# Two stacked attention layers on one core: the reciprocal row sums travel by DMA through device memory instead of through TensorE, and the normalisation comes four steps later

## The reference

```python
# layer 0
q = einsum('oc,bcn->bon', Wq, xf) + bq          # 32 rows
k = einsum('oc,bcn->bon', Wk, xf) + bk          # 32 rows
v = einsum('oc,bcn->bon', Wv, xf) + bv          # 256 rows
attn = softmax(einsum('bci,bcj->bij', q, k), axis=1)
x = gamma * einsum('bcn,bnm->bcm', v, attn) + xf
# layer 1
theta = conv1x1(x, theta_w, theta_b)            # 32 rows, 4096 positions
phi = maxpool2(conv1x1(x, phi_w, phi_b))        # 32 rows, 1024 positions
g = maxpool2(conv1x1(x, g_w, g_b))              # 128 rows, 1024 positions
attention = softmax(theta^T phi, axis=-1)
y = gamma * (out_w @ (g @ attention^T) + out_b) + x
```

## Time and profile before

| | |
|---|---|
| median of 3 executions | 2790.31 us (2786.36 to 2790.55) |
| profiled execution, own time | 2785.08 us |
| its span | 2783.3 us |
| PE busy | 2693.6 us (97%) |
| POOL busy | 1956.3 us (70%) |
| DVE busy | 2004.2 us (72%) |
| ACT busy | 1745.2 us (63%) |

### The profile page before, as it was taken

One profiled execution on the slowest core, in us unless ns is written; L12 is line 12 of the kernel. 1 busy time (PEld: TensorE's weight loads), 2 busy tenths in 40 slices (PEclk: granted clock), 3 DMA queues, 4 the chain that ended last, 5 costly groups with the idle time before them and its releaser, 6 DMA issues.

```text
span 2783.3 us, 39336 instructions
## 1 busy us (share of the span) xinstructions
PE 2693.6 (97%) x12260; PEld 2159.1 (78%) x12260; DVE 2004.2 (72%) x3303; ACT 1745.2 (63%) x3171; POOL 1956.3 (70%) x1544
## 2 busy tenths in 40 slices
PE   7999999999999999998999999999899999999988
PEld 5788888877688888887778888888767888888866
DVE  7677777767767777776776777777676777777665
ACT  5566666666756666666765566666676666666657
POOL 3677777767767767776786767777577677777768
PEclk9999999999999999999999999999999999999989
DMA  2000000012110000001211000000121000000011
GB/s 86 1 16 24 16 24 16 16 39 69 61 38 16 24 16 16 16 16 38 69 65 35 24 16 16 16 16 16 46 76 61 16 16 16 16 16 16 16 46 61
DMA packets 43194, 85.03 MB, mean 31 GB/s; under 512 B 2672, under 2 KB 2800, under 8 KB 42992
## 3 DMA queue, kind: packets, MB, share of 16 engines
q1 hardware_dynamic: 35360, 68.17, 7.2%
q10 hardware_dynamic: 7632, 14.36, 1.8%
HBM read 48.96 MB, written 33.55 MB: 30 GB/s over the span
## 4 chain that ended last, share of the span: by engine, by line
PE 87%; DVE 4%; issue 3%; ACT 3%; POOL 2%; DMA 0%; POOLq 0%; ACTq 0%; DVEq 0%
PE o_ps L821 18%; PE o_ps L824 18%; PE o_ps L825 18%; PE s_ps L798 10%; PE aux L861 9%; PE aux L835 2%; PE aux L874 2%; PE aux L870 2%; DVE mx L675 2%; PE aux L895 1%; POOL prob_l L446 1%; PE aux L839 1%; PE aux L878 1%; ACT queries L530 1%; PE o_ps L861 1%
## 5 line engine op out<-in xcount | busy, mean ns | idle before, releaser
L446 POOL TENSOR_TENSOR prob_l<-prob,prob_h 128x512 fp32r<-128x512 f32 x1280 | 1640.6, 1289 | 717.4 <-ACT prob_h L508 706.0
L505 ACT ACTIVATE prob<-s_ps 128x512 f32<-128x512 f32 x1280 | 767.3, 599 | 819.8 <-PE s_ps L798 817.2
L675 DVE TENSOR_REDUCE mx<-aux 128x1 f32<-128x512 f32 x1103 | 760.7, 690 | 424.0 <-PE aux L861 419.0
L821 PE MATMUL o_ps<-prob_h,vh 128*128 128x512 f32 x2304 | 926.8, 402 | 0.5 <-ACT prob_h L508 0.4
L824 PE MATMUL o_ps<-prob_l,vh 128*128 128x512 f32 x2304 | 904.6, 393 | 1.4 <-POOL prob_l L446 1.3
L825 PE MATMUL o_ps<-prob_h,vl 128*128 128x512 f32 x2304 | 903.1, 392 | 0.0
L637 DVE TENSOR_TENSOR acc<-prob,acc 128x512 f32<-128x512 f32 x1216 | 836.4, 688 | 26.8 <-ACT prob L505 11.4
L508 ACT ACTIVATE prob_h<-s_ps 128x512 fp32r<-128x512 f32 x1280 | 762.1, 595 | 0.0
L798 PE MATMUL s_ps<-queries,keys 128*128 128x512 f32 x1280 | 524.3, 411 | 17.9 <-DVE queries L694 10.8
L824 PEld LDWEIGHTS o_ps<-prob_l,vh 128*128 128x128 f32 x2304 | 436.7, 190 | 97.7 <-POOL prob_l L446 5.0
L825 PEld LDWEIGHTS o_ps<-prob_h,vl 128*128 128x128 f32 x2304 | 434.6, 189 | 99.7
(11 more groups left out here) (122 smaller groups left out, 1947.9 us busy)
## 6 DMA issues: line engine op xcount, KB each, us to landing
xa<-x SPq DMA_DIRECT2D x32, 512.0 KB, 3.7
spill<-xa SPq DMA_DIRECT2D x32, 512.0 KB, 2.7
xa<-spill SPq DMA_DIRECT2D x32, 512.0 KB, 3.7
y<-xa SPq DMA_DIRECT2D x32, 512.0 KB, 2.7
xp<-x ACTq DMA_DIRECT2D x26, 512.0 KB, 3.7
xp<-x SPq DMA_DIRECT2D x2, 512.0 KB, 9.1
prob<-w_in ACTq DMA_DIRECT2D x1, 576.0 KB, 5.3
wo<-w_out ACTq DMA_DIRECT2D x1, 128.0 KB, 6.1
```

Of the source, the lines that this page charges most:

```text
L446: nc.gpsimd.tensor_tensor(out=prob_l[:, i, :], in0=prob[:, i, :], in1=prob_h[:, i, :].bitcast(f32), op=ALU.subtract).then_inc(pl_ready, 1)
L505: nc.scalar.activation(prob[:, i, :], s_ps[s][:, :], ACT.Exp).then_inc(p_ready, 1)
L675: ins = nc.vector.tensor_reduce(out=dst, in_=bank[:, :], axis=AX.X, op=ALU.max)
L821: mm(o_ps[ct][:, :], value(vh, l, t, ct), prob_h[:, i, :], start=t == 0, stop=False)
```

## The change

`D2` leaves PE, except for the last chunk of layer 0 of each image and the very last chunk, which keep their bank. For the other 59 chunks SP writes `rsum` into a row in device memory (`r_rows`), waits for it, and reads the row back broadcast over 128 partitions into a new buffer `rb`. DVE multiplies in step 4 of the next chunk and waits there for the second DMA. In layer 0 all that follows (`N` to `T1L`) comes four steps later; in layer 1 the two `Z` move from steps 2 and 4 to steps 4 and 6, and `ZA` from 3 and 5 to 5 and 7. The `ST` jobs are placed anew. The new tensor `nm_rows` and its path in SP serve an `M` without a bank; the plan has none, so that path is never taken. Of the 128 columns of `nm_wide` and rows of `queries` 98 are used.

```diff
-                put(g, 1, on(Job("D2", *prev, 0), X1))
+                put(g + 4, 1, Job("D2", *prev, 0))
                 if prev[0] == 0:
-                    c = prev[2]
-                    put(g + 1, 1, Job("N", *prev, 0))
...
+                    c, h = prev[2], g + 4
+                    put(h + 1, 1, Job("N", *prev, 0))
...
                 else:
                     for k in range(CT):
-                        put(g + 3 + 2 * k, 1, on(Job("Z", *prev, k), X1))
-                        put(g + 4 + 2 * k, 1, Job("ZA", *prev, k))
+                        put(g + 5 + 2 * k, 1, on(Job("Z", *prev, k), X1))
+                        put(g + 5 + 1 + 2 * k, 1, Job("ZA", *prev, k))
             if n + 1 < NCH:
-                steps = [(i, X0) for i in range(27)] + [(i, X1) for i in range(20, 25)]
-                steps.sort()
-                for i, (t, at) in enumerate(steps):
-                    put(g + t, 1 if at == X1 else 3, maxima(0, b, n + 1, i // SUBS, i % SUBS, at))
+                steps = sorted(([(0, 1, X0), (0, 1, X1)] + [(t, 3, X0) for t in range(1, 27)]
+                         + [(t, 1, X1) for t in (20, 21, 22, 23)]), key=lambda e: e[:2])
+                for i, (t, place, at) in enumerate(steps):
+                    put(g + t, place, maxima(0, b, n + 1, i // SUBS, i % SUBS, at))
             else:
-                for i in range(SUBS * (NCH - 1)):
-                    put(g + i, 3, maxima(1, b, i // SUBS, 0, i % SUBS, X0))
+                for i, (t, place, at) in enumerate([(0, 1, X0), (0, 1, X1)] + [(t, 3, X0) for t in range(1, 27)]):
+                    put(g + t, place, maxima(1, b, i // SUBS, 0, i % SUBS, at))
...   (layer 1)
-                put(g, 1, on(Job("D2", *prev, 0), X0))
+                put(g + 4, 1, Job("D2", *prev, 0))
                 for k in range(CT):
-                    put(g + 2 + 2 * k, 3, on(Job("Z", *prev, k), X0))
-                    put(g + 3 + 2 * k, 3, Job("ZA", *prev, k))
+                    put(g + 4 + 2 * k, 3, on(Job("Z", *prev, k), X0))
+                    put(g + 5 + 2 * k, 2 * k + 1, Job("ZA", *prev, k))
...
             if n + 2 < NCH:
-                for s in range(SUBS):
-                    put(g + 4 + s, 3, maxima(1, b, n + 2, 1, s, Y))
+                for s, (t, place) in enumerate(((0, 1), (5, 3), (6, 3), (7, 3))):
+                    put(g + t, place, maxima(1, b, n + 2, 1, s, Y))
...
-                    for s, (t, place, at) in enumerate(((2, 3, Y), (3, 3, Y), (5, 3, X0), (6, 3, X0))):
+                    for s, (t, place, at) in enumerate(((0, 1 if n else 3, X0), (1, 3, X0), (2, 3, Y), (3, 3, Y))):
...   (SP)
+                elif name == "D1" and Job("D2", l, b, c, 0) in ROW_OF:
+                    i = ROW_OF[Job("D2", l, b, c, 0)]
+                    wait_free(sp, job)
+                    sp.dma_start(r_rows[row].rearrange("(s p) -> p s", p=P), rsum[:, :]).then_inc(r_out, 16)
+                    sp.wait_ge(r_out, 16 * (i + 1))
+                    wait(sp, scaled, i)
+                    sp.dma_start(rb[:, :], r_rows[row:row + 1, :].broadcast_to([P, CH])).then_inc(r_in, 16)
...
+            for g in range(TILES):
+                    for job in late.get(g, ()):
+                        reload(*job[1:4])
+                    for job in BEFORE.get(g, ()):
+                        entry(job)
+                    for e in DURING.get(g, ()):
+                        entry(e.job)
+                        if e.job.name == "ZA" and e.job.k == CT - 1:
+                            late.setdefault(g + 2, []).append(e.job)
...   (DVE, job D2)
+                    if job in BANK:
+                        wait_full(dve, job)
+                        recip, done = bank, free[BANK[job]]
+                    else:
+                        dve.wait_ge(r_in, 16 * (ROW_OF[job] + 1))
+                        recip, done = rb, scaled
...   (PE, job Z)
-                    wait_free(pe, Job("D2", l, b, c, 0))
+                    wait_scaled(pe, l, b, c)
```

More of the change, by code:

```diff
@@ L272 @@
         LAST_READ.append(Job("G1", 1, _job.b, _job.c, 0) if _job.l else Job("V0", 0, _job.b, _job.c, 1))
+    if _job.name in ("M", "D2") and _job not in BANK:
+        ROW_OF[_job] = sum(j.name == _job.name for j in ROW_OF)
     if _job.name in ("K0", "V0", "K1Q", "K1K", "T1"):
@@ L429, in _, with entry @@
                     load_a(nxt // NCH % 2, nxt // (2 * NCH), nxt % NCH)
+            def entry(job):
+                name, l, b, c, k = job
+                row = chunk_no(l, b, c)
+                if name in ("N", "ZA") and k == CT - 1:
+                    store_a(l, b, c)
+                elif name == "XL" and l == 1 and k == CT - 1:
+                    reload(0, b, c)
+                elif name == "M" and job in ROW_OF:
+                    i = ROW_OF[job]
+                    wait_free(sp, LAST_MAX[l, b, c])
+                    sp.dma_start(nm_rows[row].rearrange("h (s p) -> p s h", p=P),
+                                 nm_wide[:, :, NM].bitcast(f32)).then_inc(nm_out, 16)
+                    sp.wait_ge(nm_out, 16 * (i + 1))
+                    wait(sp, nm_in, 16 * i)
+                    sp.dma_start(queries[NM, q_slot(l, b, c), :].bitcast(f32), nm_rows[row]).then_inc(nm_in, 16)
+                elif name == "D1" and Job("D2", l, b, c, 0) in ROW_OF:
[5 more added lines that the diff above has]
+                    sp.dma_start(rb[:, :], r_rows[row:row + 1, :].broadcast_to([P, CH])).then_inc(r_in, 16)
+            for p in range(ASLOTS + PSLOTS):
+                load_p(p)
+            late = {}
+            with nc.allow_non_contiguous_dma(reason="rows of one value per partition"):
+                for g in range(TILES):
[7 more added lines that the diff above has]
+                            late.setdefault(g + 2, []).append(e.job)
+                for job in END:
+                    entry(job)
             for slot in range(ASLOTS):
@@ L682, in maximum @@
                                               op=ALU.max, negate=True))
+                stored = max((ROW_OF[j] + 1 for j in ROW_OF if j.name == "M" and chunk_no(*j[1:4]) < chunk_no(l, b, n)),
+                             default=0)
+                wait(dve, nm_out, 16 * stored)
                 chain(nc.vector.tensor_copy(nm_wide[:, :, R3], nm))
@@ L691, in entry @@
                     maximum(job)
-                elif name == "M":
+                elif name == "M" and job in BANK:
                     wait_full(dve, job)
-                    nc.vector.tensor_copy(queries[R3:P, q_slot(l, b, c), :], bank[R3:P, :]).then_inc(
+                    nc.vector.tensor_copy(queries[NM, q_slot(l, b, c), :], bank[NM, :]).then_inc(
                         free[BANK[job]], 1)
```

73 lines of the change are left out of this document (42 added, 31 removed).

## The result

The changed kernel takes 3257.32 us (median of 4 executions, 3253.33 to 3261.16) against 2788.8 us for the kernel before on the same chip, a ratio of 1.168 with a 95% interval of 1.166 to 1.170. I had forecast 2781 us, range 2755 to 2810. It is 468 us slower.

The account below looks back on a forecast made before the run. PE, busy 97% of the span, was taken to bound the kernel. Layer 0's -14.3 us and layer 1's +5.2 us make -9.1 us, from 2790.3 to 2781 us, range 2755 to 2810.

Parts of the forecast that it names:

- Added: two DMAs in series: Path of the reciprocals through device memory: hops of 2.3 and 3.0 us, some 5.5 us with waits, bounds 4.3 and 7.3.
- My sentence that hop 1's writes would have to take over 90 ns each: First hop: the prediction is wrong upwards if its element writes take over 90 ns each.
- Rival 2: Hops land late, DVE and PE wait in some 22 layer 1 chunks: 2807 us at 7.5 us latency; chance 0.20.
- decision point: Layer 1: beyond 6.3 us of hop latency DVE and PE wait one for one in some 22 chunks.
- hidden even at the upper bound: Layer 0: four steps, 7.4 us, plus 1.3 us from the reciprocal to step 0 cover the hops' latency.
- The shift of `N` to `T1L` by four steps adds no PE instruction: Layer 0: the later jobs add no PE instruction; DVE and POOL have over a quarter of the time free.
- 0.46 us: Gap left by `D2` at layer 0 boundaries: two `ST` fit there, saving 0.46 us at 31 boundaries, 14.3 us.
- The walk of layer 1: Layer 1 chunks followed job by job from `D1` on PE: changes from -1.4 to +2.2 us a chunk, sum +5.2 us.
- costed at nothing: Narrower `nm_wide` and `queries`: no cost, since a matmul's cost goes with its 512 columns.
- Rival 3: No change: layer 1 costs 25 us, less what layer 0 gives; 2790 to 2800, said 2793 us; chance 0.18.

Follow-up runs that it names:

- experiment 1: Changed kernel with `D2` back on PE, in step 4 of the next chunk, and no DMA hops; the rest of the change stays: 2923.25 us, ratio 1.049.
- experiment 5: Changed kernel with hops only in layer 0, multiplication in step 9, layer 1 as before, 128 rows and columns, no `ST` in steps 9 and 10: 2777.62 us.
- experiment 10: Kernel before with only layer 0's new order, `D2` on PE in step 4, `ST` on X1 in steps 21 to 24 instead of 20 to 23: 2799.4 us.
- Experiment 7: Kernel before with only layer 1's new order, `D2` on PE in step 4: 2867.18 us, ratio 1.028.
- experiment 6: Kernel before with only the narrowing, 98 instead of 128 rows in the score matmul and 98 columns of `nm_wide`: 2803.37 us, ratio 1.0056.
- experiment 3: Changed kernel with the second hop issued right behind the first, without waiting, reading 2 KB of the input instead of the reciprocals: 3067.73 us.
- experiment 9: Kernel before with only layer 0's new order, `D2` on PE in step 4, `ST` on X1 from step 20: 2840.87 us, ratio 1.019.

## Why the prediction was wrong, point by point

- **"Added: two DMAs in series"** is the step that failed, with 334 us of the 468. Hop 1 was 2.3 us, bound 4.2; it is 8.9 us to landing. The bound was the worst row that I had, a full packet's 91 ns for each of 32 elements an engine. By that count an element would be at (8.9 - 1.25) / 32 = 240 ns, but the form of the term was wrong and not only its size: the engines are through with the elements after 1.3 us, the same number of them 64 bytes apart lands after 2.0 us, and it is neighbours that cost. Hop 2 was 3.0 us and is 3.3 alone, 4.9 in the kernel. Together 14.1 us from reciprocal to use, not 5.5, with an upper bound of 7.3. My sentence that hop 1's writes would have to take over 90 ns each was the right alarm, and the range didn't heed it. The 2.0 us of the Trainium skill, DMA: Bandwidth & Descriptors, "Anatomy of one DMA", are given there for DMAs that GpSimd issues, and SP issues these; the 4.6 us estimated from them are as far off as my own 5.5.
- **Rival 2**, that the hops land late, named the mechanism and its place; its decision point, 6.3 us, was not tried by itself. Its slope, 22 us for each us over 6.3, gives 22 x 7.8 = 172 us at 14.1 us; between experiment 1 and the changed kernel layer 1 differs by 674 - 513 = 161 us in 28 distances. That the two agree is in part luck, for the lower clock is in the measured number and not in the slope. What it left out is layer 0, "hidden even at the upper bound": DVE there has 217.18 - 207.34 = 9.8 us of room and waits 4.23, and with the lower clock after it an inner chunk is 5.0 us longer, 24 of them 120 us.
- **"The shift of `N` to `T1L` by four steps adds no PE instruction"**: true, and it cost 41 us, by a bank. I had counted instructions and free time of the engines, and not who stands in front of whom on X1 in step 20.
- **"0.46 us" for two `ST` in the gap**: right in experiment 5 (63.7 to 63.9 against 64.3 us), and experiment 10 fits it.
- **The walk of layer 1**: right up to `attend` (2.78 and 3.12 us, walked 2.75 and 3.0). Experiment 7 has +0.9 to +2.9 us for chunks 1 to 4 of the last image where I had +0.6; less the 0.81 us of `D2` on PE, which the walk didn't have, its two chunks of 14.4 us are at +0.7, near the walk, and the one of 15.9 has the lower clock besides. For images 0 to 2 the sign of chunks 4 and 5 was right and the size was not, +6.5 and +5.0 against +2.2; chunks 6 and 7 lost 1.0 to 1.6 and 0.5 where I gave them a gain of 1.4. The whole was +5.2 and measured +79, of which 28 x 0.81 = 23 us can be `D2`, an estimate.
- **Narrowing "costed at nothing"**: 15 us. The score matmul's own distance stayed, as I had it; the term that I put at nothing is in the matmuls around it, 0.5 us in a chunk of layer 0 (experiment 6).
- **Rival 3's sum** is off by 4 us: 2790.3 - 14.3 + 25.3 is 2801 us, and with half of the gain of chunks 6 and 7 kept 2797, not 2793.

The single parts add up nearly: narrowing 15, layer 0's order 53, layer 1's order 79, in all 147 against 134 for the three together in experiment 1; where the 13 us between go was not tried. Then the hops, at least 278 us for the first one's neighbouring elements and at most 56 for what is left: the second hop and what the late multiplication costs, less `D2`'s time on PE. How the 41 of layer 0 and the 43 of layer 1 divide into the wait itself and the lower clock after it was not tried.

## What to carry to other kernels

Before a value goes through device memory, ask how its elements lie there: 512 single elements of 4 bytes as neighbours cost several times what the same number spread out, or the same bytes in larger pieces, cost, and what is issued right behind them lands with them. When a job is moved by a few steps, write down for its bank who comes right before and right after; free time on the engines says nothing about that. And put a new latency where it has room, here nine steps instead of four, and only in the layer that has them: then the little that the change can give (0.36%) is really had.

## What the hardware showed that I had not expected

- 512 neighbouring elements of 4 bytes, written from 128 partitions: 9.1 us; 64 bytes apart 2.0; in pieces of 8 bytes 3.0, of 16 bytes 2.0. A DMA issued right behind such neighbours took 9.8 instead of 3.3 us (experiment 3). The engines' packets are through after 1.3 us in both of the first two.
- DVE with a second operand in SBUF instead of PSUM, beside a busy POOL: 1263 instead of 745 ns, up to 1784, and POOL 1.70 instead of 1.29 us.
- A reciprocal of 128x512 on DVE takes 3360 ns, of 128x4 182 ns.
- After PE's first wait of 4.14 us in the changed kernel's layer 0 the granted clock is 0.56 over 3.7 us. After the waits of 1.3 us in layer 0 of the first image it stays at 1.00 (experiment 9). Of five waits of 1.16 to 1.18 us one had a lower clock behind it, 0.62 over 4.5 us, and four had 1.00 (experiment 7).
- Score matmuls over 98 instead of 128 rows were not faster, and the chunk of 32 steps took 0.5 us longer.
